# Third softmax's exponentials as stationary f16 halves, and the start-up in the order of need

## What is computed

```python
kernel1 = softmax(Q @ K_l^T)      # 1024 x 64 per head
kernel2 = softmax(Q_l @ K_l^T)    # 64 x 64
kernel3 = softmax(Q_l @ K^T)      # 64 x 1024
SV  = (kernel1 @ iterative_inv(kernel2)) @ (kernel3 @ V)   # six Newton-Schulz steps
out = SV @ w_proj
```

## Time and profile before

| | |
|---|---|
| median of 3 runs | 2302.66 us (2300.61 to 2303.02) |
| the profiled execution's own time | 2305.19 us |
| its span, first to last instruction | 2303.5 us |
| TensorE busy | 2010.8 us, 87% of the span |
| VectorE busy | 1504.5 us, 65% |
| ScalarE busy | 858.9 us, 37% |
| GpSimd busy | 676.7 us, 29% |
| mean granted TensorE clock | 0.96 of full speed |

### The profile page before, as it was taken

The page is one execution under the profiler, slowest core; times in us unless marked ns, Lnnn a source line. Parts: engine busy times, 40 slices in busy tenths (PEclk is TensorE's granted clock), DMA queues, the critical chain, the costliest instruction groups (busy, mean ns, idle before and its releaser), DMA issues.

```text
span 2303.5 us, 58849 instructions
## 1 busy us (share of the span) xinstructions
PE 2010.8 (87%) x24985; PEld 1302.1 (57%) x24985; DVE 1504.5 (65%) x3470; ACT 858.9 (37%) x1490; POOL 676.7 (29%) x902
## 2 busy tenths in 40 slices
PE   2588998989899898989989898998989899898945
PEld 2264755647475564747556474755647475564724
DVE  4376667676766767576676757667675767767542
ACT  1243443343344334334443433444343443434321
POOL 2113132331513223151323315132331513233051
PEclk7788999999999999999999999999999999999978
DMA  3323222151422215142221514222151422214020
GB/s 83 82 60 78 44 75 61 26 129 30 115 44 72 59 29 130 29 113 46 74 63 23 130 30 115 44 71 65 25 129 29 115 43 76 63 22 111 11 55 19
DMA packets 232972, 150.71 MB, mean 65 GB/s; under 512 B 153035, under 2 KB 203732, under 8 KB 232693
## 3 DMA queue, kind: packets, MB, share of 16 engines
q1 hardware_dynamic: 232710, 146.95, 27.2%
HBM read 36.98 MB, written 16.78 MB: 23 GB/s over the span
## 4 chain that ended last, share of the span: by engine, by line
PE 57%; DVE 20%; SPq 10%; issue 4%; ACT 3%; POOL 3%; DMA 2%; DVEq 1%; POOLq 0%; ACTq 0%
PE NS L905 11%; SPq L416 10%; PE ringF L1112 9%; PE ringA L1072 5%; PE KV L986 5%; PE ringA L806 4%; PE ringF L1096 4%; PE ringF L1145 3%; DVE stage L1529 2%; DVE mx L1439 2%; DVE mx L1453 2%; PE ringA L948 2%; PE ringA L972 2%; PE ringF L806 2%; PE ringF L1147 2%
## 5 line engine op out<-in xcount | busy, mean ns | idle before, releaser
L1112 PE MATMUL ringF<-x,H 128*128 128x256 f16 x1536 | 237.9, 273 | 0.0
L1453 DVE TENSOR_REDUCE mx<-ringA 128x8 f32<-128x512 f32 x256 | 175.6, 687 | 77.8 <-PE ringA L948 76.7
L651 ACT ACTIVATE E<-ringA,score_scale 128x512 f32<-128x512 f32 x256 | 175.6, 686 | 122.9 <-PE ringA L972 122.9
L806 PE MATMUL ringA<-xT,wqkv 128*128 128x512 f16 x768 | 181.3, 387 | 30.1 <-DMA KS<-KS 13.6
L1112 PE MATMUL ringF<-H 128*128 128x128 f16 x1024 | 204.4, 220 | 1.7 <-DVE H L1542 1.7
L1439 DVE TENSOR_REDUCE mx<-ringA 128x1 f32<-128x512 f32 x256 | 160.3, 684 | 47.1 <-PE ringA L939 46.5
L1096 PE MATMUL ringF<-wd,x2T 128*128 128x512 f16 x768 | 186.7, 382 | 5.0 <-DVE H L1540 3.3
L1506 DVE SCALAR_TENSOR_TENSOR X<-X,NS 128x320 f32<-128x320 f32 x160 | 78.0, 488 | 169.7 <-PE NS L905 164.5
L659 ACT ACTIVATE E<-ringA,score_scale 128x512 f32<-128x512 f32 x256 | 158.8, 685 | 69.9 <-PE ringA L1003 69.9
L469 POOL TENSOR_SCALAR vtmp<-mv,eps_ffn 128x8 f32<-128x8 f32 x16 | 5.1, 316 | 606.9 <-DVE mv L1285 606.9
L469 POOL TENSOR_SCALAR vtmp<-mv,eps_ln 128x8 f32<-128x8 f32 x32 | 9.9, 310 | 552.6 <-DVE mv L1285 544.1
(11 more groups left out here) (250 smaller groups left out, 4330.1 us busy)
## 6 DMA issues: line engine op xcount, KB each, us to landing
KS<-stage SPq DMA_DIRECT2D x384, 64.0 KB, 2.0
QS<-stage SPq DMA_DIRECT2D x384, 64.0 KB, 2.0
...
```

Of the source, the lines that this page charges most:

```text
L651: A(E[:, k % ESLOTS, :], ps[:, :], ACT.Exp, scale=score_scale[:, 0:1]).then_inc(freed["s3"].sem, 1)
L806: ins = MM(dst, left(a, k), right(c, k), start=n == 0, stop=n == 3 * KC - 1)
L1112: ins = MM(dst, H[:, a, t, own], src, start=first and i == 0, stop=last and i >= 3, skip_group_check=True)
L1453: V_.reduce_max(mx1[:, t, 8 * h:8 * h + 8], take(b, "m1", k)[:, :].rearrange("p (a m) -> p a m", a=8), AX.X)\
```

## The change

It has two parts.

**Third softmax.** The exponentials become the stationary operand, in halves of f16, and the values the moving one. `sum_values` is now, for each of four pairs, one matmul with the 128x128 `hi` tile of E against 65 columns (V's lo half, V's hi half, and a one), and one with the `lo` tile against 33 columns (V's hi half and a one). The sums come out with landmarks on the partitions, so the denominators are one column each: VectorE copies both banks out (`values_take`), takes a reciprocal of 128x8, adds two pieces and multiplies (`values_place`); `values_normalise` and `values_transpose` are gone. The first four pairs gather in the bank `KV`, the others in `NS[1]`; the small products for the inverse's start move to `KV` and `NS[0]`.

The halves are made as follows. `hi` of E: ScalarE by a second exponential from the same bank, written as f16, ahead of the f32 one, for k other than 1, 5, 9, 13; for these four VectorE by a copy (`exponentials_hi`), which stands in its list at the end of step k+2. `lo` of E: GpSimd, all 16, in order (`exponentials_lo`). Halves of V: GpSimd (`values16`), four copies and two subtractions, between `norm2(b-1)` and `exponentials_lo(b)`. `norm1(b+1)` comes behind. `sum_values` stands one step later, at k-3, and the last ones are spread around the first half of `gram` 0. The halves of E lie in `yout`; V, before its split, in slots 4 to 7 of E.

**The feed-forward's `gram`.** The doubled hi half (L1542) is gone; the product that used it goes to 128 columns of its own, which R2 weighs by two. The reduction of a gram bank is 512 columns wide instead of 384.

**Start.** w_qkv has a semaphore of its own. GpSimd makes all constants first, then the reduction for w_qkv, then `norm1(0)`. VectorE takes x's statistics first, then the maximum, scale and split of w_qkv alone (`DVE_QKV`, ten steps), for which TensorE's first batch waits. The feed-forward's set-up goes into batch 0: TensorE's parts between the first three Newton-Schulz steps (`ffn_weights`), `ffn_sums` on VectorE behind step 1, `ffn_scales` behind the thin products, the splitting of the weights on GpSimd (`ffn_weights`, ahead of `attn_residual(0)`), and `ffn_reduction` at the end of VectorE's batch 0. The two DMA copies are issued ahead of the first transposes.

```diff
-        DVE_BIAS = 12
-        DVE_SETUP = 32
+        POOL_FOLD = 3
+        POOL_EARLY = 16
+        POOL_CONSTS = 35
+        POOL_QKV = POOL_CONSTS + 1
+        POOL_FFN = POOL_QKV + 1
+        POOL_DONE = POOL_FFN + 14
+        DVE_QKV = 10
+        DVE_FFN_SUMS = 12
+        DVE_FFN_MAX = 13
+        DVE_FFN_SCALES = 18
+        DVE_SETUP = 20
...
+            def values16(b):
+                for k in range(4):
+                    rows = slice(2 * k, 2 * k + 2)
+                    pool.wait_ge(freed["pv"].sem, freed["pv"].at(b, k + 1))
+                    pool.sem_inc(s_apart, 1)
+                    if k == 0 and not first(b):
+                        pool.wait_ge(kv_full.sem, kv_full.at(b - 1, 2 * T))
+                        pool.sem_inc(s_apart, 1)
+                    pool.tensor_copy(V16[:, rows, :, HD2:2 * HD2], V[:, rows, :, :]).then_inc(v16.sem, 1)
+                for g in range(2):
+                    rows = slice(4 * g, 4 * g + 4)
+                    pool.wait_ge(v16.sem, v16.at(b, 4 + g))
+                    pool.sem_inc(s_apart, 1)
+                    pool.tensor_tensor(V16[:, rows, :, 0:HD2], V[:, rows, :, :], V16[:, rows, :, HD2:2 * HD2],
+                                       ALU.subtract).then_inc(v16.sem, 1)
+            def exponentials_lo(b):
+                for k in range(16):
+                    if k % 4 == 1:
+                        pool.wait_ge(e_hi.sem, e_hi.at(b, k // 4 + 1))
+                    else:
+                        pool.wait_ge(freed["s3"].sem, freed["s3"].at(b, k + 1))
+                    pool.sem_inc(s_apart, 1)
+                    pool.tensor_tensor(E16[:, k % 4, 1, :], E[:, k % ESLOTS, :], E16[:, k % 4, 0, :], ALU.subtract)\
+                        .then_inc(e_lo.sem, 1)
...
                 if not first(b):
                     norm2(b - 1)
+                values16(b)
+                exponentials_lo(b)
                 if more:
                     norm1(b + 1)
-                if not first(b):
+                if first(b):
...
                 ps = take(b, "s3", k)
                 if k >= ESLOTS:
-                    act.wait_ge(kv_full.sem, kv_full.at(b, k - ESLOTS + 1))
+                    act.wait_ge(e_lo.sem, e_lo.at(b, k - ESLOTS + 1))
+                elif k == 4:
+                    act.wait_ge(v16.sem, v16.at(b, 6))
+                if k % 4 != 1:
+                    if k >= 4:
+                        act.wait_ge(kv_full.sem, kv_full.at(b, k - 4 + 1))
+                    elif k == 0 and not first(b):
+                        act.wait_ge(x2lo.sem, x2lo.at(b - 1, 2))
+                    A(E16[:, k % 4, 0, :], ps[:, :], ACT.Exp, scale=score_scale[:, 0:1])
                 A(E[:, k % ESLOTS, :], ps[:, :], ACT.Exp, scale=score_scale[:, 0:1]).then_inc(freed["s3"].sem, 1)
...
             def sum_values(b, k):
                 g, t = k // T, k % T
-                pe.wait_ge(freed["s3"].sem, freed["s3"].at(b, k + 1))
+                pe.wait_ge(e_lo.sem, e_lo.at(b, k + 1))
                 if k == 0:
-                    pe.wait_ge(freed["pv"].sem, freed["pv"].at(b, 4))
+                    pe.wait_ge(v16.sem, v16.at(b, 6))
                     if not first(b):
-                        pe.wait_ge(w_done.sem, w_done.at(b - 1, 3))
-                for i in range(2):
-                    for j in range(GP):
-                        p = g * GP + j
-                        ins = MM(KV[32 * j:32 * j + 32, (2 * g + i) * P:(2 * g + i + 1) * P], onesf[:, :] if i else V[:, t, p, :],
-                                 E[:, k % ESLOTS, j * P:(j + 1) * P], start=t == 0 and i == 0, stop=t == T - 1,
-                                 skip_group_check=True)
+                        pe.wait_ge(w_done.sem, w_done.at(b - 1, 4))
+                acc_bank = (KV, NS[1])[g]
+                for j in range(GP):
+                    p = g * GP + j
+                    cols = slice(j * P, (j + 1) * P)
+                    MM(acc_bank[:, j * VW:(j + 1) * VW], E16[:, k % 4, 0, cols], V16[:, t, p, 0:VW], start=t == 0 and j == 0,
+                       stop=False, skip_group_check=True)
+                    ins = MM(acc_bank[:, j * VW + HD2:(j + 1) * VW], E16[:, k % 4, 1, cols], V16[:, t, p, HD2:VW], start=False,
+                             stop=t == T - 1, skip_group_check=True)
                 ins.then_inc(kv_full.sem, 1)
-            def values_transpose(b):
-                pe.wait_ge(w_done.sem, w_done.at(b, 2))
-                for g in range(2):
-                    ins = TR(KV[:, g * P:(g + 1) * P], Wt[:, g, :], identf[:, :])
-                ins.then_inc(wt_full.sem, 1)
...
-                    if k >= 2:
-                        sum_values(b, k - 2)
+                    if k >= 3:
+                        sum_values(b, k - 3)
...
+                sum_values(b, 13)
+                if ffn_too:
+                    gram(b - 1, 0, range(0, T // 2))
                 for k in range(14, 16):
                     sum_values(b, k)
-                if ffn_too:
-                    gram(b - 1, 0, range(0, T // 2))
-                values_transpose(b)
                 fold1_transpose(b)
                 if ffn_too:
                     gram(b - 1, 0, range(T // 2, T))
                 for k in range(5):
                     ns_first(b, k)
+                    if first(b):
+                        ffn_weights(k)
                     if ffn_too and k < 3:
...
+            pe.wait_ge(s_set.sem, 1)
             pool_tokens(0)
-            pe.wait_ge(s_set.sem, DVE_SETUP)
+            pe.wait_ge(s_set.sem, DVE_QKV)
...
-            def values_normalise(b):
-                dve.wait_ge(kv_full.sem, kv_full.at(b, 2 * T))
-                kv = KV[:, :].rearrange("p (g i n) -> p g i n", g=2, i=2)
-                V_.reciprocal(Wt[:, :, :], kv[:, :, 1, :]).then_inc(w_done.sem, 1)
-                dve.wait_ge(w_done.sem, w_done.at(b, 1))
-                V_.tensor_tensor(Wt[:, :, :], Wt[:, :, :], kv[:, :, 0, :], ALU.mult).then_inc(w_done.sem, 1)
+            def exponentials_hi(b, k):
+                dve.wait_ge(freed["s3"].sem, freed["s3"].at(b, k + 1))
+                if k >= 4:
+                    dve.wait_ge(kv_full.sem, kv_full.at(b, k - 4 + 1))
+                V_.tensor_copy(E16[:, k % 4, 0, :], E[:, k % ESLOTS, :]).then_inc(e_hi.sem, 1)
+            def values_take(b, g):
+                dve.wait_ge(kv_full.sem, kv_full.at(b, T * (g + 1)))
+                V_.tensor_copy(kvs[:, 4 * g:4 * g + 4, :], (KV, NS[1])[g][:, 0:GP * VW].rearrange("p (a n) -> p a n", a=GP))                    .then_inc(w_done.sem, 1)
             def values_place(b):
-                dve.wait_ge(wt_full.sem, wt_full.at(b, 1))
-                kv = KV[:, 0:2 * P].rearrange("p (a h d) -> p a h d", a=PAIRS, h=2)
-                V_.tensor_copy(X[0:M, :, M:XA], kv[0:M, :, 0, :])
-                V_.tensor_copy(X[M:P, :, M:XA], kv[M:P, :, 1, :]).then_inc(w_done.sem, 1)
+                dve.wait_ge(w_done.sem, w_done.at(b, 2))
+                V_.reciprocal(rden[:, :], kvs[:, :, 2 * HD2])
+                for e in range(2):
+                    rows = slice(e * M, (e + 1) * M)
+                    ins = V_.tensor_tensor(vsum[rows, :, :], kvs[rows, :, e * D:(e + 1) * D],
+                                           kvs[rows, :, HD2 + e * D:HD2 + (e + 1) * D], ALU.add)
+                ins.then_inc(w_done.sem, 1)
+                dve.wait_ge(w_done.sem, w_done.at(b, 3))
+                V_.tensor_tensor(X[:, :, M:XA], vsum[:, :, :], bcast(rden[:, :], D), ALU.mult).then_inc(w_done.sem, 1)
             def ns_linear(b, k):
...
-                values_normalise(b)
+                    if k % 4 == 3:
+                        exponentials_hi(b, k - 2)
                 fold1_rows(b)
+                values_take(b, 1)
                 values_place(b)
...
```

360 lines of the change are left out of this document (204 added, 156 removed).

## The result

The changed kernel takes 2488.98 us (median of 4 runs, 2485.01 to 2496.1), the kernel before 2302.84 beside it: ratio 1.0809, 95% interval 1.0787 to 1.0831. It is slower by 186 us; the forecast was slower by 80, and the range ended at 2435.

The account below looks back on a forecast made before the run. TensorE's own instruction row, busy 87% of the span, was taken as the bound. Start and batch 0 gave -15, 15 batches x (3.7 + 2.6) gave +94.5: together +80, 2385 us, median 2382; 8-in-10 range 2245 to 2435.

Parts of the forecast that it names:

- +3.7 a batch: At fold3: GpSimd's two value subtractions hold VectorE's tiny F3 steps, so TensorE waits; bounds 0 to 4.2 us.
- The standing before sum_values 1, 5, 9 and 13: In the loop: TensorE waits for differences behind VectorE's halves, 2.1, 1.0, 2.3 and 2.4 us, 7.8 in all.
- the pooling row: Profile row, 30 ns per matmul: eight new sum_values matmuls take 0.24 us against 0.58, giving back 5.3 us a batch.
- rival (d): Weight loads not hidden behind sum_values' matmuls: 0.78 us a step, about 6 more a batch, 2478 us; chance 0.03.
- Left out of the sum: the clock.: Lower TensorE clock after fold3's idle time: up to 1.7 us a batch in three hidden tiles, counted only in the range.
- +2.6: Loop, first maxima1 to first Newton-Schulz product: 35.9 us against 33.24, so 2.6 us more a batch; bounds +1 to +4.5.
- -37: Start: w_qkv's reduction and normalisation run early, so the first projections start near 38.3 us instead of 75.4.
- +10 and +4: Batch 0: FFN set-up between Newton-Schulz steps costs 10 us; VectorE's R2 and rcol ahead of batch 1 cost 4.
- (a): Only fold3 waits and VectorE's halves come in time: -1.2 us a batch, 2262 us; chance 0.12.
- (b): Only the loop waits and the tiny F3 instructions slip between GpSimd's: 2323 us; chance 0.10.
- (c): Neither fold3 nor the loop waits: -4.9 us a batch, 2202 us; chance 0.12.
- every 133.2 us: Reading of the kernel before: one batch follows the other every 133.2 us, from (2090.0 - 91.6) / 15.

Follow-up runs that it names:

- e2: Changed kernel with GpSimd's two subtractions of the values waiting until VectorE has made F3: 2424.2 us, ratio 1.0523.
- e9: Changed kernel with VectorE's four halves at the end of step k+1 instead of k+2: 2408.5 us, ratio 1.0468.
- e3: Changed kernel with all sixteen f16 halves made by ScalarE, none by VectorE: 2380.7 us, ratio 1.0341.
- e4: Changed kernel with unread TensorE products added, 44 ahead of fold3's transpose and 20 ahead of sum_values 1, 5, 9 and 13: 2437.7 us, ratio 1.0582.
- e8: e6 with R2 and rcol behind batch 1's first maxima3, w_qkv's maximum on TensorE instead of GpSimd, and the first normalisation ahead of later stages' constants: 2248.3 us.
- e1: Changed kernel with the third softmax of before put back, so the changed beginning alone: 2294.8 us, ratio 0.9968.
- e12: e8 with R2 and rcol back in their place and ScalarE instead of GpSimd scaling wup: 2240.0 us, ratio 0.9724.
- e6: Changed kernel with e2's and e3's edits, plus VectorE's next-batch token statistics and sum_of_squares moved out of the loop: 2261.9 us, ratio 0.9829.

## Why the prediction was right or wrong

**Right: the direction, and the mechanism of both waits.** fold3 was forecast at +3.7 a batch for GpSimd's subtractions and is 3.3; e2 removes it by order alone. The standing before sum_values 1, 5, 9 and 13 was forecast place by place at 7.8 in all and is 6.1 (6.3 with the 0.28 behind the second); e9 and e3 show that VectorE's halves in that order are its cause. The new matmuls cost what the pooling row said, so rival (d) was rightly small.

**Wrong: "Left out of the sum: the clock."** This is the step that failed. I priced it at fold3 alone, up to 1.7 a batch, and set it to nothing; there it is 1.1. But I had put 7.8 us of standing into the loop myself, and did not ask what clock TensorE's next instructions would have. The loop's end ran at 0.50, and over the whole loop the clock made TensorE's own work 6.5 us longer (31.6 against 25.2). Keeping TensorE busy gave 3.6 us a batch back net, 2.9 of it in the loop (e4): more than half of the 5.9 us by which a batch was under-forecast (12.2 against 6.3).

**The loop's sum, "+2.6", was right but for this.** It is 7.8. The standing was forecast as 7.8 and 1.5 more, less the 1.5 saved, and grew by 7.1; the matmuls were forecast as -5.3 and give -5.8 at full clock. So neither is too low in the sum, and the missing 5.2 us are the clock's. Where e4 kept the clock at 1.00, the loop took 36.6, where the prediction had followed it step by step to 35.9. The 6.5 us are not all loss: at full clock TensorE would stand for a part of them. How large that part is stays open; e4's 36.6 says 2 or less.

**Mis-sized: the start, "-37".** It is -27.5. The step "the reduction for w_qkv is then ready to run ... from there the normalisation takes what it took" had no price for the reduction itself, since the trace before hides it in a long wait for VectorE. It costs 12.8 us of gaps, and e8 shows that they go with it; the normalisation took 14.6 instead of 18.3, VectorE's splitting of w_qkv being done by then.

**Mis-sized: the FFN in batch 0, "+10 and +4".** Together 18.0 (e1). VectorE's R2 and rcol took 8.2 us, not 4, beside GpSimd's scaling of wup, and 4.6 without it (e12): the same hold that I had reckoned with at fold3.

**The rivals.** (a) and (b), one wait without the other, are not what happened; both waits are there. (c), neither wait, is what e6 builds, with VectorE relieved besides: I gave it 4.9 us a batch, the kernel gets 2.5, since TensorE then stands behind VectorE's maxima.

The forecast fell short by 106 us: 8 up to fold3 of batch 0; 8 in batch 0 (4 by the FFN's set-up, 4.5 in its loop, which grew by 9.0); 85 in the fourteen batches behind it; and 5 after the last fold3.

One reading was off without changing the sum: "every 133.2 us" takes in the short batch 0; a middle batch of the kernel before takes 134.3.
